# A three-stage decoder layer: the next batch's input transposed one attention iteration sooner, its u projections around the final sum, x_proj summed chunk by chunk

## The chip, the cores and the metric

One core of a Trainium2 chip runs the whole kernel. The metric is the device time of one launch in microseconds (us), less is better; data and weights are float32.

## What is computed

For each of 8 batches of 512 tokens by 256 features, three stages follow each other:

```python
# stage 1, Mamba block: x1 = layernorm(x + mamba(layernorm(x)))
u, z  = split(W_in @ xn)                     # 512 channels each
u     = silu(conv4(u) + conv_b)              # causal, 4 taps
dbc   = W_x @ u                              # 16 rows for dt, 16 for B, 16 for C
dt    = softplus(W_dt @ dbc[:16] + dt_bias)
h[t]  = exp(dt*A)*h[t-1] + dt*B[t]*u[t]      # 512 channels x 16 states
y     = (sum_n C[n]*h[n] + u*D) * silu(z);  out = x + W_out @ y
# stage 2, slot attention to a context of 64 rows, 3 iterations
#   rmsnorm, scores, softmax over slots, weights normalised over tokens, GRU cell with tanh and sigmoid gates
#   then x2 = rms/layer norm of (h + x1)
# stage 3, feed-forward with relu squared, 5 spike steps (counted by 5 thresholds), residual, layernorm
```

## The kernel before

Each of five engines has its instruction stream written out by hand, held together by semaphores: TensorE (PE), VectorE (DVE), ScalarE (ACT), GpSimd (POOL), and SyncE (SP), which issues all DMAs. A body works on several batches at once: stage 1 of batch i, stage 2 of batch i-1, stages 2 to 3 of batch i-2, the spikes and last norm of batch i-3. Bodies 0 and 1 lack some stages (0 has stage 1 alone), body 2 lacks the spikes; bodies 3 to 7 are full, and a `drain` ends the rest. Between bodies all engines meet (`meet`): SP waits for four arrivals, clears the semaphores and lets them go.

A body is cut in 35 positions g (`SLOTS`). In the first 32 stage 1 does on DVE one multiply of 128x1024 (line 1384) and one scan of 128x1024 (L1393), on ACT two exponentials for the decay two positions ahead (L1129), on POOL the product with C (L492), on PE 8 transposes that add up the states, two positions later (`hsum`, L769 and for the last one L756). All else is put between by `plan` (lines 290 to 324): for each engine and position a list of steps, which `take` calls in that order. An engine runs its stream strictly in order, so a step that waits holds all that stands behind it. `("mid", g)` stands between the scan and the next multiply; a plain g behind both.

Attention iteration k has a row of steps: `norm` (PE L608, L609, ACT L1032), `score` (DVE L1320), `weigh` (ACT L1038, exponentials), `soft`, `recol`, `renorm` (DVE L1326 to L1334), `gate_h`, `gate_x`, `cand_h`, `cand_x` (PE L630 to L645), their tanh on ACT (L1041, L1095), `hold` (DVE L1339), and on POOL `keep` and `cand` (L457, L461, L464), which give the new hT and count `h_done`. `sq` is its square on ACT (L1027). `up` and `down` are the feed-forward (PE L734, L742, ACT L1056, L1058).

The change touches the way of the next batch. `next_stats` (DVE, layernorm statistics of xin) stands at position 23, between `score` and `soft` of attention iteration 2; POOL makes the root at 22; `next_norm` (ACT L954) stands at 26; `turn` (8 PE transposes L543 to the two banks of px, two ACT copies L961 to xnT) at 29, behind the last candidate. `final` 0 at 30 turns hT back and adds x1 (PE L670, L674, both banks of px), ACT copies the sum to x2 (L1101), DVE takes its statistics; on DVE that step stands ahead of the last scan. Then come `u` 0 to 3 (PE L553, two matmuls of 512 columns each; ACT L966), `conv` (DVE L1267, six for each two chunks), `silu` (ACT L972), `outp` 0 to 3 (PE L715, the output projection; L1418 and L1422 finish y's last chunk), and x_proj (PE L559), which waits for all four chunks of u, and whose copy `keep_bc` (ACT L977) SP writes to DRAM for the next body's B and C (L370). Residual, statistics and norm of stage 1 end the body on DVE (L1436, L1239, L1250). The banks of u are px0, px1, pb3 and px0 again:

```python
u_banks = (px[:, 0, :], px[:, 1, :], pb[:, 3, :], px[:, 0, :])
back_bank = (pc[:], pb[:, 3, :])
```

## Time and profile before

| | us |
|---|---|
| median of 3 runs | 1699.95 |
| lowest, highest | 1696.39, 1705.75 |
| the profiled execution, its time | 1699.65 |
| its span, first to last instruction | 1697.8 |

| engine | busy us | share | instructions |
|---|---|---|---|
| PE | 1360.2 | 80% | 5536 |
| DVE | 1310.5 | 77% | 1508 |
| ACT | 989.2 | 58% | 1547 |
| POOL | 866.1 | 51% | 432 |

The mean granted clock of TensorE is 0.898. No engine is busy throughout, so the shares alone do not say what bounds the kernel: one has to read, stretch by stretch, who waits for whom. All views show one profiled execution.

### The profile page before, as it was taken

How to read it: one execution, taken by the hardware profiler on the slowest of the kernel's cores; microseconds unless marked ns; L12 is line 12 of the kernel's file. 1: busy time of each engine (PE TensorE's matmuls, PEld its weight loads, DVE VectorE, ACT ScalarE, POOL GpSimd, SP SyncE). 2: the span in 40 equal slices, each digit the busy share in tenths (PEclk: the TensorE clock that was granted, in tenths of full speed). 3: DMA queues.
4: the chain of work that ended last, by engine and by line, in shares of the span. 5: the costliest groups of instructions: out<-in, count | busy, mean ns of one | idle time of the engine just before them, and what ended most of it. 6: DMA issues, size and time to landing. Idle time of an engine off the chain costs nothing. (4 is left out here: it accounts for less than half of the span.)

```text
span 1697.8 us, 16460 instructions
## 1 busy us (share of the span) xinstructions
PE 1360.2 (80%) x5536; PEld 808.5 (48%) x5536; DVE 1310.5 (77%) x1508; ACT 989.2 (58%) x1547; POOL 866.1 (51%) x432
## 2 busy tenths in 40 slices
PE   4465787787888789887888789887888789887787
PEld 1244444454445445454445455454445455453354
DVE  2899688876887898968987888968987888973335
ACT  3644575537665576737765567737765567734522
POOL 0566257644666266644766267644766267640100
PEclk9775898797999899997999989997999989999898
DMA  4733343306332443306332343306331343300000
GB/s 165 262 134 114 140 148 112 111 25 226 123 105 70 140 161 104 118 15 225 128 115 66 128 159 111 119 17 225 126 115 68 125 162 111 116 19 2 12 0 25
DMA packets 64875, 188.96 MB, mean 111 GB/s; under 512 B 6304, under 2 KB 22560, under 8 KB 64832
## 3 DMA queue, kind: packets, MB, share of 16 engines
q1 hardware_dynamic: 64832, 188.43, 32.1%
q8 instruction: 22, 0.36, 0.1%
q14 instruction: 21, 0.17, 0.0%
HBM read 183.62 MB, written 4.78 MB: 111 GB/s over the span
## 5 line engine op out<-in xcount | busy, mean ns | idle before, releaser
L492 POOL TENSOR_TENSOR reg_a<-reg_a,cb 128x1024 f32<-128x1024 f32 (+1 forms) x256 | 600.5, 2355 | 308.3 <-DVE reg_a L1393 302.8
L1393 DVE TENSOR_TENSOR_SCAN reg_a<-reg_a,pb 128x1024 f32<-128x1024 f32 x256 | 584.8, 2284 | 27.3 <-ACT reg_a L1129 15.5
L1129 ACT ACTIVATE reg_a<-dt,neg_a 128x511 f32<-128x511 f32 x512 | 334.6, 710 | 54.1 <-DVE reg_a L1393 53.6
L769 PE MATMUL py<-ident,reg_a 128*128 128x128 f32 x1984 | 286.7, 296 | 83.3 <-POOL reg_a L492 83.3
L1384 DVE TENSOR_TENSOR pb<-bb,pb 128x1024 f32<-128x1024 f32 x256 | 314.5, 1228 | 24.4 <-DVE reg_a L1393 2.9
L769 PEld LDWEIGHTS py<-ident,reg_a 128*128 128x128 f32 x1984 | 250.3, 153 | 172.7 <-POOL reg_a L492 113.8
L630 PE MATMUL px<-hT,whh 128*128 128x512 f32 x252 | 120.2, 604 | 0.0
L457 POOL TENSOR_TENSOR xs<-xs,hT 128x1024 f32<-128x1024 f32 x24 | 56.5, 2354 | 111.5 <-ACT xs L1049 111.5
L734 PE MATMUL pc<-x2T,w_fc 128*128 128x512 f32 x192 | 99.4, 643 | 8.2 <-ACT reg_m L1056 8.2
L742 PE MATMUL pc<-w_pr,reg_m 128*128 128x256 f32 x384 | 90.9, 382 | 8.6 <-ACT reg_m L1058 8.6
L742 PEld LDWEIGHTS pc<-w_pr,reg_m 128*128 128x128 f32 x384 | 69.6, 190 | 25.7 <-ACT reg_m L1056 13.4
L1041 ACT ACTIVATE xs<-px,half_b 128x512 f32<-128x512 f32 x63 | 40.8, 681 | 70.4 <-PE pb L635 35.4
L703 PE MATMUL pc<-xnT,w_in 128*128 128x512 f32 x128 | 75.1, 717 | 7.1 <-DVE sz L1300 6.6
L446 POOL TENSOR_TENSOR post_rstd<-post_var,mhalf 128x4 f32<-128x4 f32 x8 | 8.1, 1007 | 126.7 <-DVE post_var L1244 126.7
L630 PEld LDWEIGHTS px<-hT,whh 128*128 128x128 f32 x252 | 44.3, 190 | 58.6 <-issue 57.8
L1267 DVE SCALAR_TENSOR_TENSOR u<-px,cols,u 128x509 f32<-128x509 f32 (+2 forms) x81 | 56.3, 739 | 18.8 <-ACT u L966 18.6
L461 POOL TENSOR_TENSOR xs<-xs,silu 128x1024 f32<-128x1024 f32 x21 | 49.5, 2356 | 36.8 <-ACT xs L1095 36.8
L477 POOL TENSOR_TENSOR dt<-dt,reg_y 128x512 f32<-128x512 f32 x32 | 43.7, 1386 | 47.8 <-ACT reg_y L1118 47.8
L553 PE MATMUL px<-xnT,w_in 128*128 128x512 f32 x108 | 53.0, 629 | 11.0 <-ACT x L1101 8.2
L608 PE MATMUL px<-hT,gT 128*64 128x512 f32 x84 | 44.3, 653 | 20.2 <-ACT xs L1027 16.2
L734 PEld LDWEIGHTS pc<-x2T,w_fc 128*128 128x128 f32 x192 | 35.7, 207 | 50.9 <-issue 32.4
L715 PE MATMUL pb<-w_out,reg_y 128*128 128x256 f32 x256 | 59.3, 380 | 0.2 <-DVE reg_a L1393 0.2
(255 smaller groups left out, 2337.1 us busy)
## 6 DMA issues: line engine op xcount, KB each, us to landing
bb<-bc_rows SPq DMA_DIRECT2D x256, 512.0 KB, 3.6
cb<-bc_rows SPq DMA_DIRECT2D x64, 512.0 KB, 6.3
xin<-x_in SPq DMA_DIRECT2D x9, 512.0 KB, 3.3
xs<-x_in SPq DMA_DIRECT2D x8, 512.0 KB, 3.3
x_out<-reg_m SPq DMA_DIRECT2D x5, 512.0 KB, 3.4
w_in<-w_inT_in SPq DMA_DIRECT2D x1, 1024.0 KB, 6.8
w_fc<-w_fcT_in SPq DMA_DIRECT2D x1, 1024.0 KB, 10.9
w_pr<-w_prT_in SPq DMA_DIRECT2D x1, 1024.0 KB, 13.1
```

Of the source, the lines that this page charges most:

```text
L457: pool.tensor_tensor(zh, tz, hT[:].rearrange("p a t -> p (a t)"), ALU.mult).then_inc(s["zh_done"], 1)
L492: pool.tensor_tensor(h[:, g % HR, 0:n], h[:, g % HR, 0:n], cb[:, 2 * q:2 * q + n], ALU.mult).then_inc(s["hc_done"], 1)
L630: pe.matmul(gate_bank[j], whh[:, e, j * P:(j + 1) * P], hT[:, e], start=(e == 0), stop=False)
L703: mm = pe.matmul(pc[:], w_in[:, e, (DT + c) * P:(DT + c + 1) * P], xnT[:, e], start=(e == 0), stop=(e == ET - 1))
L715: mm = pe.matmul(op_bank(i2), yv[:, c, i2 * P:(i2 + 1) * P], w_out[:, c], start=(c == 0 and i2 % 2 == 0), stop=(c == DT - 1), skip_group_c ...
L734: mm = pe.matmul(unit_bank(half, "up", j, mamba), w_fc[:, e, f * P:(f + 1) * P], x2T[:, e], start=(e == 0), stop=(e == ET - 1))
L742: mm = pe.matmul(bank[:, (i2 % 2) * E:(i2 % 2 + 1) * E], hid[:, j, i2 * P:(i2 + 1) * P], w_pr[:, half * UPS + j], start=(j == 0), stop=(j ...
L769: mm = pe.matmul(py[:, cols_], h[:, g % HR, j, cols_], ident[:], is_transpose=True, start=(q == 0 and j == 0 and i2 == 0), stop=(q == PAIR ...
L1129: ins = act.activation(d_a[:, g % DR, j, 1:], dt[:, c, 1:], ACT.Exp, scale=neg_a[:, c * NS + n + j:c * NS + n + j + 1])
L1267: dve.scalar_tensor_tensor(u2[:, c, back:], u_banks[c][:, 0:L - back], col("conv_w", c * KC + t), u2[:, c, back:], ALU.mult, ALU.add).then ...
L1384: dve.tensor_tensor(pb[:, 1:3, :], bb[:, g % HB], pb[:, 0:1, :].to_broadcast([P, 2, L]), ALU.mult).then_inc(s["mul_done"], 1)
L1393: dve.tensor_tensor_scan(h2[:, g % HR], d_a2[:, g % DR], pb[:, 1:3, :].rearrange("p a t -> p (a t)"), 0.0, ALU.mult, ALU.add).then_inc(s[" ...
```

## The change

`turn` goes from position 29 to 20, behind `up` 1 1 and ahead of attention iteration 2's `norm`, which now waits for xnT; `next_stats` goes to 10 (POOL 9), `next_norm` to 18. The four u chunks get four banks: pb3, pc, px0, px1. `u` 0 and 1 stand ahead of `final` 0 on PE, `u` 2 and 3 behind it at 32; chunk 3 is accumulated in another tile (`uth`), as the old u of chunk 3 is still read by then. `conv` is cut in steps of two instructions. On DVE `final` 0 goes from 30 to 33, behind the last scan and the first `conv`. x_proj is issued chunk by chunk, into py. ACT's tables are loaded by instructions of their own at other places: the one with silu at 31, the one with ln and exp behind `keep_bc` and no longer at the start of a body. Some other steps move by a position or two: `down` 1 1 on DVE, `up` 0 0 to 0 3 on ACT, `sp_ln` on ACT, `gate_x` 1 0 and `gate_h` 1 3 on PE, the spikes and the context's norm on DVE.

```diff
+TURN = 1

...
+
+        def u_acc(c):
+
+            return u2[:, c] if c < DT - 1 else uth[:, 0]

         back_bank = (pc[:], pb[:, 3, :])
...
-                      (15, ("down", 0, 1), ("gate_x", 1, 0), ("gate_x", 1, 1), ("gate_h", 1, 2)),
-                      (16, ("down", 0, 2), ("gate_h", 1, 3), ("gate_x", 1, 2), ("gate_x", 1, 3)),
-                      (17, ("down", 0, 3), ("cand_h", 1, 0), ("cand_h", 1, 1)), (18, ("cand_x", 1, 0)), (19, ("cand_x", 1, 1)),
-                      (20, ("up", 1, 0), ("up", 1, 1)), (21, ("norm", 2), ("gate_h", 2, 0)),
+                      (15, ("gate_x", 1, 0), ("down", 0, 1), ("gate_x", 1, 1), ("gate_h", 1, 2), ("gate_h", 1, 3)),
+                      (16, ("down", 0, 2), ("gate_x", 1, 2), ("gate_x", 1, 3)), (17, ("down", 0, 3), ("cand_h", 1, 0), ("cand_h", 1, 1)),
+                      (18, ("cand_x", 1, 0)), (19, ("cand_x", 1, 1)), (20, ("up", 1, 0), ("up", 1, 1), ("turn",)), (21, ("norm", 2), ("gate_h", 2, 0)),
-                      (27, ("down", 1, 2)), (28, ("cand_x", 2, 0), ("down", 1, 3)), (29, ("cand_x", 2, 1), ("turn",)),
-                      (30, ("final", 0), ("u", 0), ("u", 1)), (32, ("outp", 0)), (34, ("outp", 1), ("u", 2)),
-                      ("end", ("u", 3), ("outp", 2), ("outp", 3), ("xp",)))
+                      (27, ("down", 1, 2)), (28, ("cand_x", 2, 0), ("down", 1, 3)), (29, ("cand_x", 2, 1)), (30, ("u", 0), ("u", 1), ("final", 0)),
+                      (32, ("u", 2), ("u", 3), ("outp", 0)), (33, ("outp", 1)), (34, ("outp", 2), ("xp", 0), ("xp", 1)),
+                      ("end", ("outp", 3), ("xp", 2), ("xp", 3)))
-                      (1, ("sp_exp",), ("x2t", 0)), (2, ("weigh", 0), ("sp_ln",), ("x2t", 1)), (3, ("zed", 0)), (4, ("zed", 1)),
+                      (1, ("sp_exp",), ("x2t", 0), ("sp_ln",)), (2, ("weigh", 0), ("x2t", 1)), (3, ("zed", 0)), (4, ("zed", 1)),
-                      (8, ("out_norm",), ("zed", 3), ("cand", 0)), (9, ("up", 0, 0)), (10, ("sq", 1), ("norm", 1), ("up", 0, 1)), (11, ("up", 0, 2)),
-                      (12, ("up", 0, 3)), (13, ("weigh", 1)), (15, ("gate_x", 1, 0), ("down", 0, 1)),
-                      (16, ("gate_x", 1, 1), ("reset", 1), ("gate_x", 1, 2), ("gate_x", 1, 3), ("keep", 1)), (17, ("down", 0, 3)),
-                      (19, ("cand", 1), ("up", 1, 0)), (20, ("up", 1, 1), ("sq", 2), ("norm", 2)), (22, ("up", 1, 2)), (23, ("up", 1, 3)),
-                      (24, ("weigh", 2), ("keep_x2",)), (26, ("gate_x", 2, 0), ("gate_x", 2, 1), ("reset", 2), ("next_norm",)),
-                      (27, ("gate_x", 2, 2), ("gate_x", 2, 3)), (28, ("keep", 2)), (29, ("cand", 2), ("turn",)), (30, ("final", 0)),
-                      (31, ("u", 0), ("u", 1)), (33, ("silu", 0), ("silu", 1), ("u", 2), ("u", 3)), ("end", ("silu", 2), ("silu", 3)))
-        at("dve", ("start", ("spike", 0), ("spike", 1), ("spike", 2)), ("head", ("ctx", 0), ("ctx_norm",), ("spike", 3), ("spike", 4), ("spike", 5)),
-                      (1, ("score", 0)), (("mid", 3), ("soft", 0)), (3, ("recol", 0)), (("mid", 4), ("zed", 0)), (4, ("out_stats",), ("renorm", 0)),
-                      (5, ("zed", 1)), (("mid", 6), ("out_shift",)), (7, ("zed", 2), ("hold", 0)), (8, ("zed", 3)), (13, ("score", 1)),
-                      (("mid", 14), ("soft", 1)), (14, ("recol", 1), ("renorm", 1)), (("mid", 18), ("hold", 1)),
-                      (23, ("score", 2), ("next_stats",), ("soft", 2)), (24, ("recol", 2)), (("mid", 25), ("renorm", 2)), (25, ("down", 1, 1)),
-                      (("mid", 26), ("next_shift",)), (("mid", 28), ("hold", 2)), (28, ("down", 1, 3)), (30, ("final", 0)), (("mid", 32), ("conv", 0)),
-                      ("end", ("final", 1), ("conv", 2)))
+                      (8, ("out_norm",), ("zed", 3), ("cand", 0)), (10, ("up", 0, 0), ("sq", 1), ("norm", 1)), (11, ("up", 0, 1)),
+                      (12, ("up", 0, 2), ("up", 0, 3)), (13, ("weigh", 1)), (15, ("gate_x", 1, 0), ("down", 0, 1)),
+                      (16, ("gate_x", 1, 1), ("reset", 1), ("gate_x", 1, 2), ("gate_x", 1, 3), ("keep", 1)), (17, ("down", 0, 3)), (18, ("next_norm",)),
+                      (19, ("cand", 1), ("up", 1, 0)), (20, ("turn",), ("up", 1, 1), ("sq", 2), ("norm", 2)), (22, ("up", 1, 2)), (23, ("up", 1, 3)),
+                      (24, ("weigh", 2), ("keep_x2",)), (26, ("gate_x", 2, 0), ("gate_x", 2, 1), ("reset", 2)), (27, ("gate_x", 2, 2), ("gate_x", 2, 3)),
+                      (28, ("keep", 2)), (29, ("cand", 2)), (30, ("u", 0), ("u", 1), ("final", 0)), (31, ("u", 2), ("u", 3), ("gate_table",)),
+                      (33, ("silu", 0), ("silu", 1)), ("end", ("silu", 2), ("silu", 3)))
+        at("dve", ("start", ("ctx", 0), ("spike", 0), ("spike", 1), ("spike", 2), ("ctx_norm",)), ("head", ("spike", 3), ("spike", 4)),
+                      (("mid", 0), ("spike", 5)), (1, ("score", 0)), (("mid", 3), ("soft", 0)), (3, ("recol", 0)), (("mid", 4), ("zed", 0)),
+                      (4, ("out_stats",), ("renorm", 0)), (5, ("zed", 1)), (("mid", 6), ("out_shift",)), (7, ("zed", 2), ("hold", 0)), (8, ("zed", 3)),
+                      (10, ("next_stats",)), (("mid", 11), ("next_shift",)), (13, ("score", 1)), (("mid", 14), ("soft", 1)),
+                      (14, ("recol", 1), ("renorm", 1)), (("mid", 18), ("hold", 1)), (23, ("score", 2), ("soft", 2)), (24, ("recol", 2), ("down", 1, 1)),
+                      (("mid", 25), ("renorm", 2)), (("mid", 28), ("hold", 2)), (28, ("down", 1, 3)), (("mid", 32), ("conv", 0, 0)),
+                      (32, ("conv", 0, 1)), (("mid", 33), ("conv", 0, 2)), (33, ("final", 0), ("conv", 2, 0), ("conv", 2, 1), ("conv", 2, 2)),
+                      ("end", ("final", 1)))
-                      (17, ("keep", 1)), (18, ("cand", 1)), (22, ("next_stats",)), (28, ("keep", 2), ("cand", 2)), (30, ("final", 1)))
+                      (9, ("next_stats",)), (17, ("keep", 1)), (18, ("cand", 1)), (28, ("keep", 2), ("cand", 2)), (31, ("final", 1)))
-        MAMBA_STEPS = ("outp", "xp", "next_stats", "next_shift", "next_norm", "turn", "u", "conv", "silu", "sp_exp", "sp_ln", "dt", "rest", "zed")
...
-                if c == 3:
-                    pe.wait_ge(s["conv_step"], 5)
...
-            def x_proj():
-                pe.wait_ge(s["u_ready"], DT)
-                for c in range(DT):
-                    mm = pe.matmul(px[:, 1, :], w_x[:, c], u2[:, c], start=(c == 0), stop=(c == DT - 1))
-                mm.then_inc(s["xproj_full"], 1)
+            def x_proj(c):
+
+                pe.wait_ge(s["u_ready"], c + 1)
+                mm = pe.matmul(py[:], w_x[:, c], u2[:, c], start=(c == 0), stop=(c == DT - 1), skip_group_check=True)
+                if c == DT - 1:
+                    mm.then_inc(s["xproj_full"], 1)
...
+                    if mamba and k == TURN + 1:
+                        pe.wait_ge(s["xnT_ready"], ET)
...
-                        pe.wait_ge(s["n_ready"], ET * NI)
+                        pe.wait_ge(s["n_ready"], ET * (TURN + 1))
                     next_transposes()
                 elif step == "u":
                     if slots and k == 0:
+                        pe.wait_ge(s["n_ready"], ET * NI)
+                    elif k == 1:
+                        pe.wait_ge(s["ypost_done"], DT - 1)
+                        if ffn:
+                            pe.wait_ge(s["unit_read"], reads_before_slot(SLOTS))
+                    elif slots and k == 2:
                         pe.wait_ge(s["xs_done"], 1)
-                    if k == 2:
-                        pe.wait_ge(s["half_added"], 2)
                     u_proj(k)
...
-                        if mamba:
-                            pe.wait_ge(s["xnT_ready"], ET)
...
-                    x_proj()
+                    if k == 0:
+                        pe.wait_ge(s["half_kept"], 2)
+                    x_proj(k)
...
-                            if ffn:
-                                pe.wait_ge(s["unit_read"], reads_before_slot(g))
+                            pe.wait_ge(s["conv_step"], 2 * (KC - 1))
...
-                act.activation(u2[:, c], u_banks[c], ACT.Identity, scale=col("conv_w", c * KC + KC - 1),
+                act.activation(u_acc(c), u_banks[c], ACT.Identity, scale=col("conv_w", c * KC + KC - 1),
...
-                act.activation(u2[:, c], u2[:, c], ACT.Silu).then_inc(s["u_ready"], 1)
+                act.activation(u2[:, c], u_acc(c), ACT.Silu).then_inc(s["u_ready"], 1)
...
-                act.activation(xp, px[:, 1, :], ACT.Copy).then_inc(s["bc_kept"], 1)
+                act.activation(xp, py[:], ACT.Copy).then_inc(s["bc_kept"], 1)
+                act.preload_act_table_set(LN_EXP)
...
+            act.preload_act_table_set(SILU)
...
+                    if k < DT - 1:
+                        act.wait_ge(s["ypost_done"], k + 1)
+                    elif slots:
+                        act.wait_ge(s["nz_done"], NI)
+                    u_start(k)
+                elif step == "gate_table":
+                    act.preload_act_table_set(SILU)
+                elif step == "silu":
                     if k == DT - 1:
                         act.wait_ge(s["half_added"], 2)
-                    else:
-                        act.wait_ge(s["ypost_done"], k + 1)
-                    u_start(k)
-                elif step == "silu":
-                    if slots and k == 0:
-                        act.wait_ge(s["h_done"], NI)
                     u_silu(k)
...
-                if mamba or slots:
-                    act.preload_act_table_set(LN_EXP)
...
-            def conv(c0):
-
-                for t in range(KC - 1):
-                    for c in (c0, c0 + 1):
-                        if t:
-                            dve.wait_ge(s["conv_step"], 3 * c0 + 2 * t + c - c0 - 1)
-                        else:
-                            dve.wait_ge(s["uacc_ready"], c + 1)
-                        back = KC - 1 - t
-                        dve.scalar_tensor_tensor(u2[:, c, back:], u_banks[c][:, 0:L - back], col("conv_w", c * KC + t), u2[:, c, back:],
-                                                 ALU.mult, ALU.add).then_inc(s["conv_step"], 1)
+            def conv(c0, t):
+
+                back = KC - 1 - t
+                for c in (c0, c0 + 1):
+                    if t:
+                        dve.wait_ge(s["conv_step"], 3 * c0 + 2 * t + c - c0 - 1)
+                    else:
+                        dve.wait_ge(s["uacc_ready"], c + 1)
+                    dve.scalar_tensor_tensor(u_acc(c)[:, back:], u_banks[c][:, 0:L - back], col("conv_w", c * KC + t), u_acc(c)[:, back:],
+                                             ALU.mult, ALU.add).then_inc(s["conv_step"], 1)
```

## Rows read from the trace of the kernel before

**Rows 1.** The profile page's first line.
```profile
span 1697.8 us, 16460 instructions
```
**Rows 2.** Timeline of SP: start us, us, instruction; the first DMA of two bodies.
```profile
958.12 0.40 SPq L387 DMA_DIRECT2D xin<-x_in  x1
...
1149.22 0.41 SPq L387 DMA_DIRECT2D xin<-x_in  x1
```
**Rows 3.** Timeline of DVE, end of body 5: start, us, work, idle before and its releaser.
```profile
1116.92 1.23 DVE L1384 TENSOR_TENSOR pb<-bb,pb 128x1024 f32<-128x1024 f32 x1
1123.12 1.41 DVE L1239 BATCH_NORM_STATS2 x_st<-x 128x6 f32<-128x256 f32 x4 [4.97 <-ACT x L1101]
...
1125.08 2.29 DVE L1393 TENSOR_TENSOR_SCAN reg_a<-reg_a,pb 128x1024 f32<-128x1024 f32 x1
...
1141.75 1.41 DVE L1436 TENSOR_TENSOR xs<-xs,pb 128x256 f32<-128x256 f32 x4
...
1146.21 1.38 DVE L1250 TENSOR_SCALAR x<-xs,post_mv,post_rstd 128x256 f32<-128x256 f32 x4 [1.12 <-POOL post_rstd L446]
```
**Rows 4.** Timeline of PE, final sum of body 2, then the same stretch.
```profile
545.91 1.89 PE L674 MATMUL px<-x,ident 128*128 128x256 f32 x8
...
1112.82 1.09 PE L543 MATMUL px<-ident,st 128*128 128x128 f32 x8 [0.78 <-ACT xs L1095]
...
1117.67 1.97 PE L670 MATMUL px<-ident,hT 128*128 128x128 f32 x8 [2.90 <-POOL hT L464]
1119.44 2.53 PE L674 MATMUL px<-x,ident 128*128 128x256 f32 x8
...
1137.38 3.62 PE L715 MATMUL pb<-w_out,reg_y 128*128 128x256 f32 x16
1142.54 3.70 PE L559 MATMUL px<-u,w_x 128*128 128x512 f32 x8 [1.54 <-ACT u L972]
```
**Rows 5.** Timeline of ACT, the same stretch.
```profile
1131.90 1.28 ACT L972 ACT_TABLE_LOAD   x1
...
1146.28 0.60 ACT L977 ACTIVATE reg_a<-px 128x512 f32<-128x512 f32 x1 [3.79 <-PE px L559]
```
**Rows 6.** Timeline of POOL, the same stretch.
```profile
1117.58 4.66 POOL L492 TENSOR_TENSOR reg_a<-reg_a,cb 128x1024 f32<-128x1024 f32 x2
```
**Rows 7.** Timeline of DVE, middle of body 5.
```profile
1036.97 0.16 DVE L1326 RECIPROCAL sums<-sums 128x1 f32<-128x1 f32 x1 [0.99 <-ACT ex L1038]
...
1081.13 1.39 DVE L1239 BATCH_NORM_STATS2 next_st<-xin 128x6 f32<-128x256 f32 x4
...
1084.98 0.16 DVE L1326 RECIPROCAL sums<-sums 128x1 f32<-128x1 f32 x1 [1.84 <-ACT ex L1038]
```
**Rows 8.** Timeline of ACT, middle of body 5.
```profile
1027.82 1.32 ACT L1129 ACTIVATE reg_a<-dt,neg_a 128x511 f32<-128x511 f32 x2
...
1113.51 1.45 ACT L961 ACTIVATE xnT<-px,cols 128x512 f32<-128x512 f32 x2 [0.75 <-PE px L543]
```
**Rows 9.** Timeline of PE, middle of body 5.
```profile
1070.63 1.09 PE L769 MATMUL py<-ident,reg_a 128*128 128x128 f32 x8 [2.54 <-POOL reg_a L492]
```
**Rows 10.** Timeline of DVE, body 0's end and body 1's head.
```profile
183.65 0.75 DVE L1267 SCALAR_TENSOR_TENSOR u<-pb,cols,u 128x509 f32<-128x509 f32 x1 [2.43 <-ACT u L966]
...
200.95 0.70 DVE L1374 TENSOR_TENSOR pb<-dt,u 128x512 f32<-128x512 f32 x1 [4.09 <-POOL dt L477]
```
**Rows 11.** Timeline of PE, ahead of the first body.
```profile
33.05 6.49 PE L559 MATMUL px<-u,w_x 128*128 128x512 f32 x8 [4.94 <-ACT u L972]
```
**Rows 12.** Windows, body 5 to body 6's head: stretch, us, PE, PEld, DVE, ACT, POOL busy, PEclk, DMA.
```profile
1037.00:1058.00 21.00, 20.79 (x93) 13.24 (x93) 16.47 (x14) 13.71 (x20) 11.39 (x6) 1.00 0.31 100
...
1117.00:1122.00 5.00, 4.29 (x16) 3.53 (x16) 1.15 (x1) 0.00 (x0) 5.00 (x3) 0.66 0.34 105
...
1172.00:1182.00 10.00, 9.54 (x31) 6.75 (x30) 7.43 (x8) 7.87 (x14) 8.65 (x6) 0.50 0.59 213
1182.00:1192.00 10.00, 10.00 (x43) 5.58 (x42) 7.85 (x15) 5.36 (x8) 3.25 (x3) 0.99 0.19 65
```

14 lines of the change are left out of this document (9 added, 5 removed).

## The prediction

> **What bounds the kernel now.** I read the times first: the profiled execution took 1699.65 us against a median of 1699.95, with a span of 1697.8 [rows 1]. So 1.9 us lie around the span, and the sum below is made against 1699.65 and raised by 0.3. The first DMAs of two neighbouring bodies are 191.1 us apart [rows 2]: that is a full body, and there are five such (3 to 7). A gain of 1 us in a full body is 0.3% of the kernel. The chain of waits in the page is too merged to help, so I followed the timelines of the four engines through body 5 and asked at each idle gap who ended it.
>
> The bound changes several times in a body. Where DVE runs its multiplies and scans without a gap, it sets the pace. Where it waits, a chain of small steps on PE and ACT does: at `soft` 1 it idles 0.99 us for ACT's exponentials, at `soft` 2 1.84 us [rows 7]. At the body's end a single chain decides: hT is ready at 1117.6 [rows 6], PE turns it and adds x1, ACT copies, DVE takes statistics, and only then comes the last scan, at 1125.08, 7 us after its multiply had ended (1116.92 + 1.23) [rows 3 to 5]. Behind it stand the last sum over states, the last chunk of y, two u chunks, `outp` 3, then residual and norm, whose last step starts at 1146.21 [rows 3]. In parallel x_proj waits for the last silu and its copy ends at 1146.9 [rows 4, 5]. Both ends come within 1 us of each other, so both must move.
>
> **The end of a body.** I laid the new order over the rows, from 1117.67, where PE may turn hT.
> - PE is free at 1112.8 now that `turn` has left, and does the states' sum (1.09) [rows 9] and `u` 0 and 1 (as 8 pieces of 512 columns, 3.70) [rows 4]: done at 1117.6, in a gap of 2.90 us plus the 1.09 of `turn`. They cost nothing; without that gap they would cost 3.7.
> - `final` 0 takes 1117.67 to 1121.97. The granted clock of this stretch is 0.66 [rows 12], a mix of 1.2 and 2.4 GHz, after PE had stood idle. In body 2 the second half, here 2.53, took 1.89, and 8 transposes took 1.09 ahead of the gap [rows 4], so at 2.4 GHz it is 3.0 us less their overlap of 0.1, 2.9. With `u` 0 and 1 ahead PE does not idle, and I take the fast price: done at 1120.6, 1.4 earlier.
> - The scan follows its multiply: 1118.1 to 1120.4. POOL is busy with two products until 1122.24 [rows 6], PE then sums the 31st pair until 1123.3, does `u` 2 and 3 (3.7, the copy to x2 being long done), `outp` 0 (16 pieces in 3.62, so 1.8), the last sum (1.0), `outp` 1 (1.8), y's last transposes (0.7), `outp` 2 (1.8), two chunks of x_proj (3.70 / 2 = 1.85), `outp` 3 (1.8), two more chunks (1.85): 1123.3 + 3.7 + 1.8 + 1.0 + 1.8 + 0.7 + 1.8 + 1.85 + 1.8 = 1137.8 for `outp` 3 and 1139.6 for x_proj. So PE bounds this stretch, where it used to wait.
> - DVE does 12 conv steps of at most 0.75 [rows 10] and 2 us of statistics (1123.12 to the scan at 1125.08) between 1121 and 1132, and is ready for y's last chunk. The residual's four adds take 1.41, and the first can start with half of `outp` 3 done, at 1136.9. From the first add to the last step it was 1146.21 - 1141.75 = 4.46 [rows 3], so the last step starts at 1141.4 instead of 1146.2. **The end gains 4.8 us.** The x_proj copy ends at about 1140.3 instead of 1146.9 and is hidden.
>
> In body 2 `final` already ran at the full clock, so I take 3.5 there. Body 0 has no `final` and no early gap; what it can win is the 2.43 us that DVE waits for ACT's third u chunk [rows 10], less what the conv steps ahead of y's last chunk cost: I take 2.2, bounds 0 and 3.
>
> **The middle of a body.** Here the change gives time back.
> - The statistics' 2 us stood at 1081.13 in a wait: `soft` 2 still idled 1.84 us behind them for ACT [rows 7]. Taking them away saves nothing, that wait becomes 3.8. At position 10 DVE has no gap, so `score` 1 comes 2.0 us later. But `soft` 1 waited 0.99 for ACT, so DVE alone would move it by 1.0. On ACT `up` 0 1 now comes behind its decay (1.32), which delays relu, the next `up` on PE and so `weigh` 1, less a short idle gap of ACT: I estimate 1.1 from the 1.32 [rows 8]. Both meet: +1.1. Bounds: 0.99 of idle time absorbed, 1.0, and nothing absorbed, 2.0.
> - `turn` at 20 finds PE waiting 2.54 us for POOL [rows 9] and needs 1.09 of it. ACT's two copies (1.45) [rows 8] stand ahead of relu and of `sq` 2; the transposes must come first. I get `norm` 2 0.6 us later, and with it ACT's chain to `soft` 2. Bounds: 0 and 1.09 + 1.45 = 2.5. `next_norm` (2 us on ACT) lands in a gap ahead of the tanh, and the POOL root in its idle time.
> - `down` 1 1 one position sooner frees pc for PE: -0.2.
>
> Sum: **the middle loses 1.5 us**, bounds -0.2 and +4.3. In body 1 ACT has idle time for `turn`, but DVE is the bound in position 10: +2.0. Body 0 has no attention: DVE's work only changes its place, 0.
>
> **The head.** ACT's table load (1.28, the same as at 1131.90) [rows 5] leaves the start. In full bodies DVE has the spikes to do and gains next to nothing: 0.1. In bodies 1 and 2 DVE waits 4.09 us for dt [rows 10], which comes at the end of ACT's chain; PE's first product then is the later one, so 0.9 of the 1.28.
>
> In the Trainium skill, "ScalarE: Activation LUTs", section "What ACT_TABLE_LOAD costs", a load is followed by a drain of some 1380 ns, 2.66 us in all. The row of the load [rows 5] shows 1.28 and agrees with the page's load, and it shows no drain; by the page's 2.66 bodies 1 and 2 would gain 1.4 us more each and the result would be some 3 us lower.
>
> **Ahead of the first body** x_proj's four chunks run from 33.05 for 6.49 us [rows 11]. Two of them can go while u 2 and 3 are made: -3.2. DVE then waits for the DMA of B, which starts later than everything else, so the head of body 0 gains nothing more.
>
> **The sum**: full bodies 5 x (-4.8 + 1.5 - 0.1) = -17.0; body 2 -3.5 + 1.5 - 0.9 = -2.9; body 1 -4.8 + 2.0 - 0.9 = -3.7; body 0 -2.2; start -3.2. Together -29.0: 1699.65 - 29.0 + 0.3, about **1671 us**, -1.7%.
>
> **The rivals.**
> - The end gains more and the middle costs nothing (DVE and ACT absorb it): 1.5 us better in six bodies and 2 in one, 11 in all: 1660. For it speaks that PE and DVE both idle in places [rows 7, 9]; against it that those waits hang on chains which DVE itself starts late. Chance 0.12.
> - The middle takes it back: nothing is absorbed, 4.3 us instead of 1.5 in six bodies, so 17 us worse: 1688. It decides from 2.8 us of slip. `score` 1 heads a chain through PE, which is busy for 20.79 of the 21 us from 1037 to 1058 [rows 12], and whatever it starts late stays late. Chance 0.15.
> - The change does not do what it says at the end: PE's longer queue (u 2 and 3, `outp` 0 and 1 ahead of y's last transposes) holds the last chunk, or DVE is held in its conv steps, and the residual moves by only 2 us. Then full bodies gain 0.6 and the whole some 14: 1686 to 1692. Chance 0.13.
> - Slower: the clock. PE ends the body at 1139.6 and idles until the next one starts, as far behind DVE's last step as now (1149.2 - 1146.2 = 3.0) [rows 2, 3], at about 1144.4: 4.8 us, where it now idles from 1146.2 (1142.54 + 3.70) [rows 4]. In the next head the granted clock is 0.50 from 1172 to 1182 and 0.99 from there on, while PE is busy all 10 us [rows 12]. If the longer pause shifts the return to 2.4 GHz behind that stretch, its 10 us become up to 20 and a body loses 10 - 3.4 = 6.6 us: 1700 + 7 x 6.6, about 1745. It decides from 3.4 us of slow work in the head. Against it: the clock already falls in the head of every body and comes back. Chance 0.06.
>
> The Trainium skill, "TensorE: Matmul & The Clock Gate", section "Why this matters for your kernels", warns of idle gaps of PE between bursts of matmuls. By that rule the longer pause between bodies speaks for the last rival, and the closed gap ahead of `final` for my fast price.
>
> **How the numbers follow.** Forecast as summed: 0.54. A measurement of this kernel can tell about 0.5% (8.5 us) from no change. Faster: 0.54 + 0.12 + the parts of the second and third rival below 1691.5 (0.14) = 0.80; same 0.14; slower 0.06. The range takes in the two rivals of smaller gain and the one of larger: 1654 to 1692.
>
> **What would show it.** Right: in the profile after, the last scan of a body directly behind its multiply; `final` in 2.9 us at clock 1.0; `outp` 3 and x_proj interleaved and a period of about 187.8 us between first DMAs. `soft` 1 some 1 us later from the body's start, `soft` 2 with an idle gap near 3.8 us. Wrong: a period above 190, a gap on PE ahead of y's last transposes, DVE busy with conv when they come, or a clock of 0.5 past the first third of the body.

## The result, and the profile after

The changed kernel takes 1696.09 us (median of 20 executions, 1673.31 to 1698.87) against 1701.31 us of the kernel before beside it (20 executions, 1695.92 to 1708.60). The ratio is 0.9912, with a 95% interval of 0.9887 to 0.9937: 0.9% faster, where 1.7% was forecast, and the median lies above the forecast range. That ratio leaves out six of the changed kernel's twenty executions, those of 1698.48 us and more, which count as slow; the two medians alone are 0.3% apart. The executions of the changed kernel lie 25 us apart, and their spans go with the mean granted clock: 1671.5 us at 0.906, 1687.8 at 0.893, 1696.2 at 0.889. Those of the kernel before lie 13 us apart. The profiled execution took 1695.17 us; it is one of the many long ones.

The page's first line and the first DMAs of two bodies, as in [rows 1, 2]:

```profile
span 1693.4 us, 16477 instructions
```
```profile
950.67 0.40 SPq L393 DMA_DIRECT2D xin<-x_in  x1
...
1141.82 0.41 SPq L393 DMA_DIRECT2D xin<-x_in  x1
```

Body 5 takes 191.15 us, against 191.10 before. Nothing was won in a full body, although the end of it is much shorter. The end on DVE, to be read beside [rows 3] (start us, us, work, idle time before it and who ended it):

```profile
1115.58 1.23 DVE L1397 TENSOR_TENSOR pb<-bb,pb 128x1024 f32<-128x1024 f32 x1
1116.90 2.29 DVE L1406 TENSOR_TENSOR_SCAN reg_a<-reg_a,pb 128x1024 f32<-128x1024 f32 x1
1119.22 2.23 DVE L1419 TENSOR_TENSOR reg_a<-reg_a,cb 128x512 f32<-128x512 f32 x1
1121.38 0.73 DVE L1279 SCALAR_TENSOR_TENSOR u<-pb,cols,u 128x509 f32<-128x509 f32 x1
...
1134.67 1.55 DVE L1449 TENSOR_TENSOR xs<-xs,pb 128x256 f32<-128x256 f32 x4 [0.67 <-PE pb L727]
...
1139.27 1.38 DVE L1263 TENSOR_SCALAR x<-xs,post_mv,post_rstd 128x256 f32<-128x256 f32 x4 [1.12 <-POOL post_rstd L452]
```

The last scan follows its multiply at once, the residual adds start 17.8 us after it (before: 16.7 us after a scan that itself stood 7 us late). The same stretch on PE, beside [rows 4]:

```profile
1111.56 1.90 PE L557 MATMUL pb<-xnT,w_in 128*128 128x512 f32 x4
1113.30 1.88 PE L557 MATMUL pc<-xnT,w_in 128*128 128x512 f32 x4
1116.34 1.09 PE L680 MATMUL px<-ident,hT 128*128 128x128 f32 x8 [1.16 <-POOL hT L470]
1117.27 1.89 PE L684 MATMUL px<-x,ident 128*128 128x256 f32 x8
...
1135.26 1.88 PE L563 MATMUL py<-u,w_x 128*128 128x512 f32 x4
1141.69 1.19 PE L704 MATMUL pb<-reg_a,w_dt 16*128 16x512 f32 x1 [4.55 <-SPq L424]
```

`u` 0 and 1 fill the gap ahead of `final`, `final` takes 2.82 us (1116.34 to 1119.16), and x_proj ends at 1137.1, well ahead of DVE.

So the time went elsewhere. I cut a body at four marks of SP's and DVE's timelines: its first DMA, its 6th scan, its 31st scan, the next body's first DMA. The stretch up to the 6th scan is called the head, the one behind the 31st the end, the one between them the middle. Scans are counted from one. Body 5, us:

| kernel | head | 6th to 31st scan | end | body |
|---|---|---|---|---|
| before | 37.74 | 118.67 | 34.69 | 191.10 |
| after | 38.84 | 123.68 | 28.63 | 191.15 |

The end gave 6.06, the head took 1.10 and the middle 5.01. The heads of bodies 1 to 3 took more, 2.4, 2.7 and 2.8. In the middle four stretches differ: 11th to 16th scan 24.08 before and 25.97 after, 16th to 20th 18.93 and 20.20, 23rd to 24th 4.38 and 6.32, 24th to 31st 38.29 and 38.08; the rest is equal to 0.1.

Outside the full bodies: the first DMA of body 0 came 7.5 us sooner (34.89 instead of 42.41), bodies 0 to 6 together are 0.1 longer, and what follows the first DMA of body 7 is 3.0 us longer (360.42 after 1332.98, instead of 357.42 after 1340.38): -7.5 + 0.1 + 3.0 = -4.4, the difference of the two spans.

### The profile page after: what moved, and what is told of

Read it like the earlier page. It is cut to its first block and busy times, and to the rows that moved or that the text cites. A ratio compares the mean times of both kernels' runs of the same rounds, so it can differ in the third digit from the quotient of the medians.

```text
span 1693.4 us, 16477 instructions
## 1 busy us (share of the span) xinstructions
PE 1375.6 (81%) x5536; PEld 817.3 (48%) x5536; DVE 1326.2 (78%) x1508; ACT 992.2 (59%) x1548; POOL 872.3 (52%) x432
## 5 line engine op out<-in xcount | busy, mean ns | idle before, releaser
L498 POOL TENSOR_TENSOR reg_a<-reg_a,cb 128x1024 f32<-128x1024 f32 (+1 forms) x256 | 608.3, 2384 | 368.9 <-DVE reg_a L1406 368.4
L1406 DVE TENSOR_TENSOR_SCAN reg_a<-reg_a,pb 128x1024 f32<-128x1024 f32 x256 | 585.0, 2285 | 35.9 <-ACT reg_a L1142 22.3
L781 PE MATMUL py<-ident,reg_a 128*128 128x128 f32 x1984 | 293.9, 299 | 82.2 <-POOL reg_a L498 81.4
L781 PEld LDWEIGHTS py<-ident,reg_a 128*128 128x128 f32 x1984 | 254.5, 155 | 173.8 <-POOL reg_a L498 108.2
L746 PE MATMUL pc<-x2T,w_fc 128*128 128x512 f32 x192 | 95.1, 618 | 11.2 <-ACT reg_m L1069 11.2
L715 PE MATMUL pc<-xnT,w_in 128*128 128x512 f32 x128 | 78.8, 748 | 6.4 <-DVE sz L1313 6.4
L616 PE MATMUL px<-hT,gT 128*64 128x512 f32 x84 | 51.1, 742 | 23.9 <-ACT xs L1040 19.9
L1099 ACT ACTIVATE sz<-pc 128x512 f32<-128x512 f32 x32 | 19.0, 595 | 69.6 <-PE pc L715 69.6
L727 PEld LDWEIGHTS pb<-w_out,reg_y 128*128 128x128 f32 x256 | 47.4, 190 | 12.6 <-issue 7.7
L623 PE MATMUL px<-sums,ex 64*128 64x1 f32 x168 | 28.9, 290 | 29.9 <-DVE sums L1339 29.9
```

The lines of the kernel that those rows point to most:

```text
L498: pool.tensor_tensor(h[:, g % HR, 0:n], h[:, g % HR, 0:n], cb[:, 2 * q:2 * q + n], ALU.mult).then_inc(s["hc_done"], 1)
L616: pe.matmul(px[0:M, 0, :], gT[:, e], hT[:, e], start=(e == 0), stop=(e == ET - 1))
L715: mm = pe.matmul(pc[:], w_in[:, e, (DT + c) * P:(DT + c + 1) * P], xnT[:, e], start=(e == 0), stop=(e == ET - 1))
L727: mm = pe.matmul(op_bank(i2), yv[:, c, i2 * P:(i2 + 1) * P], w_out[:, c], start=(c == 0 and i2 % 2 == 0), stop=(c == DT - 1), skip_group_c ...
L746: mm = pe.matmul(unit_bank(half, "up", j, mamba), w_fc[:, e, f * P:(f + 1) * P], x2T[:, e], start=(e == 0), stop=(e == ET - 1))
L781: mm = pe.matmul(py[:, cols_], h[:, g % HR, j, cols_], ident[:], is_transpose=True, start=(q == 0 and j == 0 and i2 == 0), stop=(q == PAIR ...
```

## The experiments

Theory A: the middle gives the end's gain back by fixed delays (the statistics at position 10, the turn at 20, the order of PE). Its first rival, theory B: the granted clock decides the length of a body. The edits are shortened to the steps that move. The first four kernels ran beside executions of the kernel before with a median of 1696.66 us.

**Statistics and turn late again.** `TURN = 2`, with the changed kernel's end kept.

```diff
-TURN = 1
+TURN = 2
-(20, ("up", 1, 0), ("up", 1, 1), ("turn",))              # PE; back to 29, as are ACT's copies
-(10, ("next_stats",)), (("mid", 11), ("next_shift",))    # DVE; back to 23 and mid 26
```

> The changed kernel with the early part undone: statistics, norm and transposes of the next batch stand where they stood before (positions 23, 26, 29), the new end (four u banks, u 0 and 1 ahead of the final sum, scan ahead of its statistics, x_proj in chunks) stays. Theory A, the middle's order gives the gain back (5 us a full body by the two traces): without it a full body takes 186 to 188 us instead of 191.15, less 1 to 2 us because u 0 and 1 no longer fit wholly ahead of the final sum, so 1663 to 1675. Theory B, the clock holds the body's length: what one part saves returns as work at 1.2 GHz in the next body, so the period stays at 190.5 to 191.5 and the time at 1690 to 1698.

Measured: 1671.13 us (1667.49 to 1671.58), ratio 0.9847 (0.9819 to 0.9875). The number is theory A's, but the reason isn't wholly: in body 5 the 11th to 13th scans are back at 4.18 and 3.70 us apart, and yet the middle takes 123.29 us. The bodies differ: 185.75 us for body 4 and 189.90 for body 5. The one has a head of 35.52 us and a middle of 121.58, the other a head of 37.95.

**Statistics and turn early alone.** The kernel before with these steps where the change has them, its end as it was.

```diff
+TURN = 1
+(20, ("up", 1, 0), ("up", 1, 1), ("turn",))
+(10, ("next_stats",)), (("mid", 11), ("next_shift",))
```

> The kernel before with the early part alone: statistics at position 10, norm at 18, transposes at 20, the end unchanged but for the missing transposes. Theory A: 4 to 5 us more in each full body, 1720 to 1735. Theory B: the body's length moves less than the positions do, 1700 to 1710, in one or more of the executions.

Measured: 1722.57 us (1722.38 to 1723.90), ratio 1.0152 (1.0123 to 1.0181). Body 5: 38.23 + 121.13 + 35.17 = 194.53. The middle loses 2.46 us with PE's old order: 24.08 to 25.97 in the 11th to 16th scan, 4.38 to 4.88 in the 23rd to 24th. The time is in theory A's range. The early steps cost, and the new end is what pays for them.

**Statistics at 14.** The changed kernel, DVE's statistics behind `recol` 1, where it waits 2.43 us for PE in the changed kernel (`spread`, L628), and the shift at 16.

```diff
-(10, ("next_stats",)), (("mid", 11), ("next_shift",)),
-(14, ("recol", 1), ("renorm", 1)),
+(14, ("recol", 1), ("next_stats",), ("renorm", 1)), (("mid", 16), ("next_shift",)),
```

> The changed kernel with only the next batch's statistics moved on, from position 10 to 14, into the 2.4 us that DVE waits for the spread sums of attention iteration 1, and the shift from 11 to 16. Theory A: the 3 us (2.0 of statistics, 1.16 of a shift that lasts 1.30 instead of 0.14) leave DVE's path, of which soft 1 had absorbed 1.1, so about 2 us a full body and 1683 to 1687 for a run of the slow-clocked kind that the profile shows. Theory B: within 2 us of the changed kernel.

Measured: 1665.34 us (1664.42 to 1665.65), ratio 0.9811 (0.9783 to 0.9839). This is 20 us below what I had expected, and body 5 says where it is not: the middle takes 123.46 us, as in the changed kernel; the head takes 35.55 instead of 38.84. But in bodies 2, 3 and 7 of the same profile the middle takes 120.8 us; the late shift, below, shows why.

**PE busy at the body's end.** Four matmuls of 512 columns, whose result nobody reads, behind the last chunk of x_proj.

```diff
                     x_proj(k)
+                    if k == DT - 1:
+                        for n in range(4):
+                            pe.matmul(px[:, 0, :], w_in[:, 0, 0:P], xnT[:, 0], start=True, stop=True, skip_group_check=True)
```

> The changed kernel with four more matmuls of 512 columns, whose results nobody reads, on PE behind the last x_proj of a body, where PE idles 4.55 us; they take 3.5 us. Theory B: the clock no longer falls at the start of the body (now 0.64 and 0.50 in its first 10 us), dt is ready sooner, and the body's slow stretches shift: 1 to 3 us a body, 1675 to 1688. Theory A: no change beyond 3 us, as PE is not the bound in the head.

Measured: 1679.66 us (1677.51 to 1679.91), ratio 0.9893 (0.9864 to 0.9922). That is in theory B's range. PE's pause between two bodies falls from 4.55 to 1.11 us. In body 5 the head takes 34.60 us; in bodies 4 and 6 it takes 38.32 and 38.22. The clock differs between them: behind 20 us it is down for 3.4 us in body 5 (22.0 to 25.4 after the first DMA) and for 6.8 in the others (26.6 to 33.4 in body 4).

All this points to the head. Its granted clock, behind the first return to 1.00, in windows of the kernel before, the changed kernel, and the one with the late shift that is told of next (columns: stretch, its length, busy time of PE, PEld, DVE, ACT, POOL with their instructions, PEclk, DMA share, GB/s):

```profile
980.50:991.00 10.50, 10.06 (x34) 7.14 (x33) 7.83 (x9) 8.25 (x15) 9.15 (x6) 0.51 0.65 212
```
```profile
973.00:984.00 11.00, 9.70 (x38) 7.14 (x37) 7.38 (x8) 8.25 (x15) 9.66 (x6) 0.54 0.55 196
```
```profile
962.50:968.00 5.50, 4.30 (x25) 3.94 (x26) 4.44 (x5) 5.41 (x12) 4.01 (x2) 0.69 0.61 207
968.00:978.00 10.00, 10.00 (x46) 5.89 (x46) 9.02 (x17) 6.42 (x10) 6.74 (x5) 1.00 0.48 164
```

From 22 to 23 us after the body's first DMA, behind an idle gap of PE of 2.75 us, the clock falls to 1.2 GHz. In both given kernels it stays there until about 33 us, in the third only until about 26 us. That is a slow patch of 10 us or of under 4, with the same program.

**Controls and single edits.** The changed kernel again; the shift alone moved; PE's old order alone; both with the statistics at 14. The kernel before had a median of 1700.66 us beside them.

> The changed kernel once more, nothing edited, beside the three kernels sent with it. Its executions so far lie between 1673.3 and 1698.9 us, and the shorter ones are those with the higher granted clock (span 1671.5 at 0.906, span 1693.4 at 0.889). Theory A (the middle of the body gives time back by fixed delays, the clock is a second effect on top): a median between 1680 and 1697, spread over more than 10 us. Theory B (the granted clock decides the length of a body, so that both kernels come to the same period of 191.15 us): the same spread, and the period of a body 191.1 to 191.2 whenever the clock is below 0.895.

Measured: 1697.71 us (1673.01 to 1699.01, 12 executions), ratio 0.9934 (0.9898 to 0.9969). The same spread, the same body: 38.86 + 123.66 + 28.63. The profiled one's first DMA came at 38.37, not at 34.89, so 3.5 us of the 7.5 at the start vary from one execution to the next.

```diff
-(10, ("next_stats",)), (("mid", 11), ("next_shift",)),
+(10, ("next_stats",)),
-(14, ("recol", 1), ("renorm", 1)),
+(14, ("recol", 1), ("renorm", 1)), (("mid", 16), ("next_shift",)),
```

> The changed kernel with one step moved: the shift of the next batch's norm (one small product with two tensors as operands) goes from the middle of DVE's position 11 to the middle of position 16; the statistics stay at 10. Theory A: beside POOL's 2.37 us operation the shift takes 1.30 us instead of 0.14, and that is 1.16 us on DVE's own chain in each of 7 bodies; moved to where POOL is quiet it takes 0.14, the 12th scan comes 1.1 us sooner, and the kernel gets 4 to 8 us shorter than the one resent beside it. Rival: the following multiply (also with two tensors) then waits for POOL in its place, and nothing is gained: within 3 us. Theory B (clock): within 3 us as well, with the 12th scan sooner and the rest of the body later.

Measured: 1669.56 us (1666.51 to 1674.69), ratio 0.9815 (0.9788 to 0.9843), by the medians 28 us less than the changed kernel instead of 4 to 8. The shift in the changed kernel, first in its place and with the POOL operation that runs at that time, then all its durations there and in this kernel (min/median/max in ns):

```profile
1018.66 2.37 POOL L498 TENSOR_TENSOR reg_a<-reg_a,cb 128x1024 f32<-128x1024 f32 x1
```
```profile
1017.54 2.29 DVE L1406 TENSOR_TENSOR_SCAN reg_a<-reg_a,pb 128x1024 f32<-128x1024 f32 x1
1019.75 1.30 DVE L1269 SCALAR_TENSOR_TENSOR next_sh<-next_mv,next_rstd 128x4 f32<-128x4 f32 x1
1020.98 1.22 DVE L1397 TENSOR_TENSOR pb<-bb,pb 128x1024 f32<-128x1024 f32 x1
```
```profile
L1269 DVE SCALAR_TENSOR_TENSOR next_sh<-next_mv,next_rstd x9: 164/1311/1348, 7.4 to 1402.0; 128x4 f32<-128x4 f32 x9
```
```profile
L1269 DVE SCALAR_TENSOR_TENSOR next_sh<-next_mv,next_rstd x9: 135/135/162, 7.5 to 1406.1; 128x4 f32<-128x4 f32 x9
```

The shift ends with POOL's operation (1021.05 and 1021.03). Theory A's price of 1.16 us is nearly right: moved, the 12th and 13th scan are 3.71 apart instead of 4.74. But from the 15th to the 16th scan it then takes 0.8 us more (7.82, before 7.02), and the middle is 123.49 instead of 123.68. In body 5 nearly the whole gain is in the head, 35.56 instead of 38.84. Body 6 of the same profile shows what hid the rest. It has the same head, 35.56, and a middle of 121.18. Two windows, from 64 us after the body's first DMA (on the way to the 16th scan) and from 115 (ahead of the 24th), in body 5 and then in body 6:

```profile
1004.50:1008.00 3.50, 3.50 (x7) 1.18 (x4) 3.33 (x2) 2.30 (x4) 3.50 (x3) 0.51 0.03 12
1055.60:1059.20 3.60, 3.56 (x9) 0.88 (x9) 3.25 (x2) 1.19 (x1) 3.60 (x3) 0.53 0.48 146
```
```profile
1192.20:1195.70 3.50, 3.42 (x16) 1.61 (x12) 3.31 (x3) 2.77 (x5) 3.50 (x3) 1.00 0.01 4
1243.40:1247.00 3.60, 3.60 (x16) 1.60 (x13) 2.51 (x2) 2.75 (x5) 3.60 (x2) 1.00 0.38 141
```

With the clock up at both places the middle is 0.84 us shorter than the 122.02 of the changed kernel with its clock up there, too (the table below). So the edit did act on the path that I had moved it for; in most bodies two new slow patches in the middle took that back, and the shorter patch in the head gave far more than I had reckoned.

```diff
-(15, ("gate_x", 1, 0), ("down", 0, 1), ("gate_x", 1, 1), ("gate_h", 1, 2), ("gate_h", 1, 3)),
-(16, ("down", 0, 2), ("gate_x", 1, 2), ("gate_x", 1, 3)),
+(15, ("down", 0, 1), ("gate_x", 1, 0), ("gate_x", 1, 1), ("gate_h", 1, 2)),
+(16, ("down", 0, 2), ("gate_h", 1, 3), ("gate_x", 1, 2), ("gate_x", 1, 3)),
```

> The changed kernel with TensorE's positions 15 and 16 in the order of the kernel before (down 0 1 ahead of gate_x 1 0, gate_h 1 3 back to position 16). Theory A: the stretch from the 15th to the 19th scan takes 18.9 us in the two kernels with the old order and 20.2 in the three with the new one, because down 0 1 comes later; with the old order it is 18.9 again, 1.27 us less in each of 6 bodies, so 5 to 8 us shorter than the changed kernel resent beside it. Rival: the 1.27 us come from the copies and the relu on ScalarE or from the earlier turn, then the stretch stays at 20.2 and the time within 2 us. Theory B (clock): the stretch shrinks and the body does not, within 3 us.

(This expectation counts scans from zero: its 15th to 19th are the 16th to 20th here.) Measured: 1667.34 us (1659.52 to 1668.78), ratio 0.9796 (0.9765 to 0.9827), again far more than the 5 to 8 us expected. The stretch is 18.93 again, so the order does cost 1.27 us. What DVE waits for there, in the changed kernel and in this one:

```profile
1053.47 0.76 DVE L1352 SCALAR_TENSOR_TENSOR pb<-pb,cols,xs 128x512 f32<-128x512 f32 x1 [2.12 <-PE pb L647]
```
```profile
1038.17 0.76 DVE L1352 SCALAR_TENSOR_TENSOR pb<-pb,cols,xs 128x512 f32<-128x512 f32 x1 [0.84 <-PE pb L647]
```

DVE waits for PE's `cand_h` 1 0, and PE is busy all the way there; so I looked for where its work got longer. `gate_x` 1 0 and 1 1 use 64 rows of the array each. In the changed kernel `down` 0 1 stands between them, here they are neighbours (rows of PE, the changed kernel first):

```profile
1037.50 1.12 PE L643 MATMUL px<-ex,vw 64*128 64x512 f32 x2
1038.55 1.99 PE L754 MATMUL pc<-w_pr,reg_m 128*128 128x256 f32 x8
1040.48 1.12 PE L643 MATMUL pb<-ex,vw 64*128 64x512 f32 x2
```
```profile
1025.18 0.69 PE L643 MATMUL px<-ex,vw 64*128 64x512 f32 x1
1025.18 0.69 PE L643 MATMUL pb<-ex,vw 64*128 64x512 f32 x1
```

As neighbours they start together and the pair takes 1.1 us, apart 1.12 each: 1.1 of the 1.27 us. The Trainium skill, "TensorE: Matmul & The Clock Gate", section "Part 3: Packing small matmuls — row/col tiling", has this rule, that matmuls on different rows of the array run side by side; the trace agrees. The head of body 5 again: 35.54; that of body 6 is still 38.80.

> The changed kernel with the statistics moved from position 10 to 14 and the shift to 16 (which alone came to 1665 us) and TensorE's old order at positions 15 and 16. Theory A: the two add up, 1665 less 6 x 1.27 = 7.6, so 1656 to 1660, and no body over 187 us. Rival: at position 14 DVE waits for ScalarE at the second softmax anyway, and the later statistics already fill the hold that TensorE's order makes; then it stays at 1663 to 1667. Theory B (clock): whatever is freed comes back as work at the half clock, 1663 to 1670 with a granted clock below 0.90.

Measured: 1660.94 us (1658.46 to 1663.05), ratio 0.9767 (0.9744 to 0.9790). Body 5 takes 184.67 us, body 4 188.85, with a head of 39.12. I had expected 1656 to 1660 and no body over 187. By the medians it is 4 us below the statistics at 14 alone and 6 below the old order alone, by the ratios 7.5 and 5, with intervals of some 5 us each way: whether the edits add up fully can't be read from the times. In the middle of a body they do: 120.82 us with the statistics at 14 (body 3), 119.54 with both (body 3, too), the order's 1.27. The heads again differ from body to body.

**Theory C: the patch in the head.** Theory A had met its numbers only in part, so I formed another. Three different edits far from the head had taken 3.3 us out of it. Either its slow patch depends on what PE does there, and its length on small shifts of the phase; or (theory D) any disturbance breaks a pattern that repeats from body to body. To tell them apart I gave PE work in the very gap of 2.75 us, in both given kernels, in the best one, and as a control the same work in another gap.

```diff
                     mm.then_inc(s["x2_full"], 1)
+                    if k == 0:
+                        pe.wait_ge(s["sp_abs"], 3)
+                        for n in range(5):
+                            pe.matmul(py[:], w_in[:, 0, 0:P], xnT[:, 0], start=True, stop=True, skip_group_check=True)
```

> The changed kernel with nothing moved; TensorE gets five matmuls of 512 columns whose result nobody reads (2.4 us at 2.4 GHz), in the idle gap of 2.75 us between the two turns of x2 in the head, where it waits for ScalarE's copy, in every body with the feed-forward part. What is known so far: in body 5 the granted clock falls from 1.00 to 0.50 some 22 to 23 us after the body's first DMA in both kernels and returns at 33 us, while in the three kernels at 1667 to 1670 us it returns at 25.5 to 26 us; there the stretch from the 5th to the 6th scan takes 7.5 us and not 9.9. Theory C (the changed kernel is worth the forecast of some 1671 us, and the missing 20 to 25 us are the 7 to 8 us of half clock in the head, which any small shift of the phase can shorten): with the gap filled the clock stays at 1.00 there, the scan comes 2.4 to 3.3 us earlier in each full body, 1668 to 1678 us, and the executions lie within 12 us of each other instead of 26. Theory A (fixed delays of the middle alone: the statistics, the shift, TensorE's order): unchanged, 1690 to 1698, or some us more for the added work.

Measured: 1667.22 us (1666.74 to 1677.50), ratio 0.9836 (0.9812 to 0.9861), beside 1698.83 of the kernel before. The gap in the changed kernel, then the same place with the five matmuls and the clock there:

```profile
969.35 0.60 PE L692 MATMUL pc<-ident,x 128*128 128x128 f32 x4
972.71 0.66 PE L692 MATMUL pc<-ident,x 128*128 128x128 f32 x4 [2.75 <-ACT x2T L1119]
```
```profile
959.54 0.60 PE L692 MATMUL pc<-ident,x 128*128 128x128 f32 x4
959.98 4.46 PE L697 MATMUL py<-xnT,w_in 128*128 128x512 f32 x10
964.27 0.60 PE L692 MATMUL pc<-ident,x 128*128 128x128 f32 x4
```
```profile
959.00:973.00 14.00, 13.00 (x61) 7.98 (x60) 12.17 (x14) 13.24 (x21) 8.82 (x6) 1.00 0.68 227
```

The five take 4.46 us, not the 2.4 that I had reckoned: they hold PE 1.7 us beyond the gap, and it still pays. In body 5 the patch is gone. In bodies 3 and 4 a shorter one of 3.4 us stands at 29 us, and the head takes 37.2; in body 6 there is none and it takes 35.55. Adding useless work made the changed kernel 29 us shorter by the medians, 13 us by the ratios (0.9912 and 0.9836). Both spread over 10 us and more, so neither figure is sharp.

> The kernel before with the same five matmuls in the same gap of 2.75 us of its head. Theory C, if the slow patch costs the kernel before as much: about 20 us shorter, 1678 to 1685 us, so that the change is worth some 8 us between kernels of a like clock. Theory C, if the kernel before loses little by the patch (its scans 5 and 6 lie 10.4 us apart, too): 1695 to 1700 us, and the change is worth its 25 us or more between kernels of a like clock. Theory A: 1700 us or a little more.

Measured: 1680.30 us (1676.57 to 1682.05), ratio 0.9884 (0.9868 to 0.9901). The clock of the kernel before with the same edit:

```profile
965.00:981.00 16.00, 15.69 (x74) 9.75 (x73) 14.42 (x23) 13.85 (x23) 12.12 (x7) 1.00 0.74 260
```

Body 5: 34.34 + 118.67 + 34.72 = 187.73. The patch cost the kernel before 3.40 us in a full body, too, and it alone. So between kernels with the gap filled the change is worth 13.1 us of 1680 by the medians, 0.8%, and 0.5%, some 8 us, by the ratios (0.9884 and 0.9836); two of the five executions of the changed one took 1677 us.

> A control: the changed kernel with the same five matmuls in another idle gap of TensorE, of 3.03 us, ahead of the second attention iteration's norm, 63 us after the body's first DMA, where the granted clock is 1.00 before and after. If the patch in the head goes away because TensorE is busy just there (theory C), this stays with the changed kernel: 1690 to 1698 us with executions down to 1673. If any disturbance of the kernel is enough to leave the slow pattern (theory D: the pattern repeats from body to body only because each is exactly as long as the last), it comes to 1665 to 1680.

Measured: 1694.13 us (1671.84 to 1696.22, 12 executions), ratio 0.9956 (0.9929 to 0.9982). The head takes 39.13 us, and a patch stands in it:

```profile
974.00:980.50 6.50, 5.96 (x16) 3.80 (x17) 3.87 (x5) 3.89 (x6) 6.50 (x5) 0.55 0.67 214
```

The control is not free of side effects (the middle loses 1.6 us at the second softmax, and wins as much at the third, where the clock stays up), and the patch of body 5 isn't the one of the changed kernel: the clock stays up behind the gap of 2.75 us and falls at 27.1 us, behind a second idle stretch of PE of 2.3 us, for 6.8 us. In bodies 6 and 7 it falls at 23.5, for 10. But a disturbance of this size, with the same work, left the kernel with long heads. Theory D falls in the form in which any disturbance is enough.

> The kernel with the statistics at position 14, the shift at 16 and TensorE's old order at positions 15 and 16 (1661 us), with the five matmuls in the gap of its head. Its clock falls there as well, from 22.7 us to 26 us, 3.4 us of half clock. Theory C: that is 1 us or so in a full body, so 1652 to 1658 us. If the short patch is hidden behind DVE's work, within 3 us of 1661; if the clock then falls somewhere later in its place, as in the kernel with the late turn (at 65 us), the same or up to 1668.

Measured: 1648.29 us (1644.59 to 1651.99), ratio 0.9695 (0.9680 to 0.9711), the fastest of all, 48 us below the changed kernel by the medians, and below the 1652 to 1658 expected. Body 5: 35.71 + 119.54 + 28.62 = 183.87.

## Why the prediction was wrong

The step that failed is the middle of a full body: forecast to lose 1.5 us, it lost 3.35 with the clock equal and 5.01 in the profiled executions. The head, put at a gain of 0.1, lost 1.1. Body 5 in all that matters, with the 23rd to 24th scan apart, where `norm` 2 is in the path:

| kernel | head | 6th to 31st scan | of it 11th to 16th | 16th to 20th | 23rd to 24th | end | body |
|---|---|---|---|---|---|---|---|
| before | 37.74 | 118.67 | 24.08 | 18.93 | 4.38 | 34.69 | 191.10 |
| before, gap filled | 34.34 | 118.67 | 24.07 | 18.93 | 4.39 | 34.72 | 187.73 |
| after | 38.84 | 123.68 | 25.97 | 20.20 | 6.32 | 28.63 | 191.15 |
| after, gap filled | 36.62 | 122.02 | 25.96 | 20.20 | 4.89 | 28.63 | 187.27 |
| best, gap filled | 35.71 | 119.54 | 24.76 | 18.93 | 4.89 | 28.62 | 183.87 |

- **The end: right, and too small.** -4.8 forecast, -6.06 measured, in every kernel that has it. The order on PE was the one laid out, and every step that I named is in the rows. From hT ready to the end of x_proj I had reckoned 21.9 us (1117.67 to 1139.6); it took 20.8 (1116.34 to 1137.1). One wrong term is the pieces of `outp` and x_proj at 1.8 to 1.85: the rows' durations overlap, and start to start they stand 1.72 apart (1133.54 and 1135.26 for two of them), eight times 0.1. That brought DVE's last step 0.8 us nearer to hT than reckoned. The other 0.45 lies behind that step: from it to the next body's first DMA it took 3.0 us before and 2.55 now, and I had reckoned with 3.0.
- **The middle: the failed step.** +1.5 forecast; +3.35 with the clock equal (118.67 to 122.02). Of this 1.9 lie from the 11th to the 16th scan. With only the shift moved away that stretch takes 25.12 in body 6, where the clock is up: so the statistics at position 10 cost 1.04, forecast 1.1, and the shift 0.84. The turn at 20 cost 0.6, forecast 0.6 (11.12 to 11.22 in the 20th to 23rd scan, 4.39 to 4.89 in the 23rd to 24th; both are undone in body 4 of the kernel with the late turn). Behind the 24th scan 0.4 came back, forecast 0.2. So the prices that I had set were nearly right, and two are missing. PE's order at positions 15 and 16 costs 1.27 us, most of it because it parts two matmuls that ran side by side; it stands in the diff and I did not weigh it at all. And the shift, a product of 128x4 elements, I had put at nothing: it takes 1.30 us beside POOL.
- **The same middle, the clock.** A second failed step. In the changed kernel `norm` 2 runs at a granted clock of 0.66, and DVE's 24th scan comes 1.4 us later than in the kernel with the gap filled; with its aftermath that is 123.68 - 122.02 = 1.66 us. I had considered the clock only ahead of `final` and in the head.

```profile
1068.00:1072.50 4.50, 3.97 (x15) 1.27 (x12) 4.22 (x3) 2.24 (x4) 4.50 (x3) 0.66 0.34 117
```
```profile
1075.11 2.29 DVE L1406 TENSOR_TENSOR_SCAN reg_a<-reg_a,pb 128x1024 f32<-128x1024 f32 x1 [2.69 <-ACT reg_a L1142]
```
```profile
1060.60 2.29 DVE L1410 TENSOR_TENSOR_SCAN reg_a<-reg_a,pb 128x1024 f32<-128x1024 f32 x1 [1.27 <-ACT reg_a L1146]
```

- **The head: wrong sign.** -0.1 forecast, +1.10 measured, and +1.2 where the long patch is absent from both (34.34 before, 35.55 in body 6 of the changed kernel with the gap filled). The table load's gain is there at the first scan (9.17 us from the first DMA instead of 10.42) and gone at the third (19.60 instead of 18.93). That is about the load's own 1.28 us. The larger 2.66 that the prediction set beside it is not borne out, as in the kernel before ACT's next instruction starts 0.01 us behind the load at 1131.90. The fourth rival had the cause, but not the place: PE now pauses 4.55 us between bodies (forecast 4.8), and the first 13 us of the next one run at 0.50, where it had run so only from 5.6 to 12.4 us:

```profile
950.67:963.50 12.83, 9.02 (x30) 4.77 (x30) 12.26 (x12) 10.42 (x22) 3.64 (x3) 0.50 0.78 301
```

  The rival let the slow stretch last beyond 33 us; the clock returned there as before. Its price was too high as well, 1.2 us a full body and not 6.6; that DVE's work covers the rest is my reading. With PE's pause cut to 1.11 us by added matmuls the head of body 5 took 34.60 us, even with a short patch in it; that is shown. I gave this rival 0.06 as a thing that is or is not; it should have been a term of the sum.
- **Full body**: forecast -3.4; the terms measured are -6.06 + 3.35 + 1.2 = -1.5 at an equal clock, and the 1.66 of `norm` 2 make it +0.1, as 191.15 against 191.10 shows. That the two came out alike is a coincidence of these sums. The -1.5 is what body 6 of the two kernels with the gap filled shows (187.74 and 186.19); in their bodies 3 and 4, where the changed one keeps a short patch, they are equal within 0.1.
- **Bodies 0 and 1, the start.** Body 0: -2.2 forecast, +0.3 measured; its end gained 1.8 (23.11 to 21.33 from the last scan), but the statistics cost 2.6 at position 10 and gave back 1.8 at 23, and 1.1 were lost from the 9th to the 10th scan, a stretch that is as long in the kernel before with its gap filled; "only changes its place, 0" was wrong. Body 1: -3.7 forecast, +0.4 measured. Body 2: -2.9 forecast, -0.2 measured. Their ends gained more than forecast (6.5 and 4.9, forecast 4.8 and 3.5), but their heads lost 2.4 and 2.7 instead of gaining 0.9, and body 1's middle lost 4.5 instead of 2.0. Start: -3.2 forecast, -4.0 between executions whose first DMAs are at 42.41 and 38.37, -7.5 with the first profiled one of the changed kernel, at 34.89.
- **Signs that I had written down.** Right: the scan behind its multiply, `final` in 2.8 us, `soft` 2 with a gap near 3.8 (4.00). Wrong: `soft` 1, which came 3.0 us later from the body's start and not 1 (81.9 against 78.9), and the period, 191.15 instead of 187.8; that was named as a sign of failure, and it was one. The second rival (1688) comes closest in time, but not by its mechanism: the statistics and the turn were absorbed about as forecast, and the loss came from steps that it did not price.
- **What the forecast number is.** Executions of the changed kernel at 1673 to 1677 us exist, and my sum of 1671 us lies near them. That is luck: the delays that I did not price stand in the middle of every profiled full body of this kernel, and also in the one with the gap filled and the clock up. None of these executions was profiled, so that they are the ones with the short patch is argued from their clock (0.900 to 0.906), not shown.

What stays open: why the patch lasts 10 us in some bodies and under 4 in others. Shown is only that PE's work in the gap removes it or shortens it; as the five matmuls also run 1.7 us past the gap, their filling it and their shifting what follows were not told apart. Kernels whose bodies start PE's work a few tenths of a microsecond sooner or later fall on either side, and I found no rule that would have told beforehand. The 3.0 us that the changed kernel loses behind the first DMA of body 7 were not followed up; with the gap filled in both it gains 2.2 us there (351.9 against 354.1), so they are no fixed delay.

On DVE and POOL the row comes first: 1.30 us instead of 0.14 beside a POOL product, with both ending together. The Trainium skill, "SBUF — State Buffer", section "SBUF: two separate sides", says that a DVE instruction with two operands in SBUF and a GpSimd instruction share a pair of ports that one of them holds for its whole length, while the other stands still. The trace agrees. So does the last y product, whose code the change leaves alone: 0.69 us in the kernel before (`L1406`), where it starts 0.05 us ahead of POOL's product, and 2.23 in the changed one (`L1419`), where it starts in the middle of one of POOL's three. DVE's multiply with one operand in PSUM takes 1.23 us beside POOL and without.

## What to carry to other kernels

Before trusting a sum of path lengths, cut the loop body at fixed marks and list for each stretch the granted clock; then ask which idle gap of TensorE lies ahead of each slow patch. Where one stands on the path, fill the gap with matmuls that nobody reads, as a first experiment: here five of them were worth 13, 18 and 29 us of 1700 in three kernels by the medians, where the change itself gave 5. And an experiment that meets its expected number has not shown its reason until the stretch it was meant to act on has moved by it: two of mine (the late turn, the late shift) gained mostly in the head. Read that stretch in several bodies, as the clock can hide in one what another shows.

## What the runs showed of the hardware that I had not expected

- One program, on one core, ran between 1673 and 1699 us, with a granted clock of 0.906 to 0.884. With the gap filled it ran between 1667 and 1677.
- A slow patch behind the same gap of PE lasts 10 us in one kernel (980.5 to 991 at 0.51) and under 4 in the next (962.5 to 968 at 0.69). In a loop it can repeat: bodies 5 and 6 of both given kernels agree within 0.06 us, patch and all. In other kernels it does not: 185.75 us and 189.90 for bodies 4 and 5 with the late turn.
- The gap of PE ahead of it is 2.75 us. In body 5 of every kernel that did not fill it the clock fell within 1.5 us behind it, at 22.0 to 23.3 us, except in the one with the late turn (28.1) and the control (27.1). The prediction named the rule of the Trainium skill against idle gaps between bursts of matmuls ("TensorE: Matmul & The Clock Gate", section "Why this matters for your kernels") for the pause between bodies and for the gap ahead of `final`. In this gap the traces show the same thing, though it is shorter than the gaps that the page warns of.
- Two matmuls of 64 rows each cost 1.1 us as neighbours and 2.2 us with another one between them.
- A DVE product of 128x4 elements takes 0.14 us or 1.30 us, depending on a POOL operation that it shares no data with.
